# Layer 2 head attention: from scores kept once to two sets of scores

## The reference

```python
x = x + _L2_attn_ref(_layernorm(x, axis=-1), L2_attn_Wq, L2_attn_Wk, L2_attn_Wv, L2_attn_Wo)
...
q, k = _rope(q, k)
scale = 1.0 / np.sqrt(Dh)
scores = jnp.einsum('bqhd,bkhd->bhqk', q, k) * scale
causal = jnp.triu(jnp.ones((S, S), dtype=bool), k=1)
scores = jnp.where(causal, -jnp.inf, scores)
attn = jax.nn.softmax(scores, axis=-1)
out = jnp.einsum('bhqk,bkhd->bqhd', attn, v).reshape(B, S, H * Dh)
return out @ Wo.T
```

## Time and profile before

| | |
|---|---|
| median of 3 runs | 1747.39 us (1744.67 to 1747.46) |
| the profiled execution | 1748.18 us |
| its span | 1746.5 us, 27918 instructions |
| granted TensorE clock, mean | 0.881 |
| PE / DVE / ACT / POOL busy | 76% / 54% / 53% / 23% of the span |
| stage L2a | from 927.0 us to 1149.3 us of the span |

### The profile page before, as it was taken

How to read it: one execution, slowest core, us unless ns; L and a number is a source line. 1 busy time by engine, 2 the same in 40 slices (tenths; PEclk the granted TensorE clock), 3 DMA queues, 4 the chain that set the end, 5 groups by cost and what they waited for, 6 DMA issues and landing times. The chain is left out here.

```text
span 1746.5 us, 27918 instructions
## 1 busy us (share of the span) xinstructions
PE 1328.2 (76%) x9137; PEld 830.3 (48%) x9137; DVE 949.7 (54%) x3708; ACT 927.3 (53%) x2185; POOL 399.7 (23%) x490
## 2 busy tenths in 40 slices
PE   5887888868899999777996878765083567877574
PEld 3555555545444444553563555454063434444464
DVE  4577777754455655445113776647222757666432
ACT  2688878752477776532421766643020467767232
POOL 5433333210311110100004332001544042210134
PEclk9899999988999999887998888886596889999687
DMA  7900000000000000000005000000122000000022
GB/s 210 135 1 2 2 2 1 2 1 1 1 1 1 1 1 1 1 1 1 1 1 178 1 1 2 1 1 11 54 74 79 2 19 14 7 14 1 8 59 78
DMA packets 60263, 42.34 MB, mean 24 GB/s; under 512 B 13188, under 2 KB 54120, under 8 KB 60120
## 3 DMA queue, kind: packets, MB, share of 16 engines
q1 hardware_dynamic: 54752, 32.42, 7.8%
q0 software_dynamic: 3552, 7.33, 1.2%
q10 hardware_dynamic: 1816, 0.81, 0.2%
HBM read 25.88 MB, written 14.66 MB: 23 GB/s over the span
## 5 line engine op out<-in xcount | busy, mean ns | idle before, releaser
L792 ACT ACTIVATE L0a_e<-L0a_e,L0a_neg_max 128x256 f32<-128x256 f32 (+1 forms) x512 | 195.5, 446 | 27.2 <-DVE L0a_neg_max L868 26.4
L679 PE MATMUL L0a_psE<-ident,L0a_e 128*128 128x128 f32 x768 | 119.0, 286 | 58.8 <-DVE L0a_probs L877 42.1
L679 PEld LDWEIGHTS L0a_psE<-ident,L0a_e 128*128 128x128 f32 x768 | 87.3, 145 | 100.8 <-issue 58.7
L1216 DVE CUSTOM_DVE_ANT_0 L3x_e<-L3x_psS,L3x_mask_rows 128x256 f32<-128x256 f32 x256 | 93.4, 420 | 70.2 <-PE L3x_psS L1076 70.0
L1164 ACT ACTIVATE L3x_e<-L3x_e,L3x_neg_max 128x256 f32<-128x256 f32 x256 | 112.6, 503 | 19.1 <-DVE L3x_neg_max L1216 19.1
L792 ACT ACTIVATE L2a_e<-L2a_e,L2a_neg_max 128x128 f32<-128x128 f32 (+1 forms) x256 | 97.3, 445 | 41.4 <-DVE L2a_neg_max L868 41.4
L1084 PE MATMUL L3x_psE<-ident,L3x_e 128*128 128x128 f32 x512 | 76.6, 284 | 47.3 <-DVE scores_L_experts_L L1226 37.1
L868 DVE CUSTOM_DVE_ANT_0 L0a_e<-L0a_psS,trinity 128x128 f32<-128x128 f32 (+1 forms) x256 | 76.3, 353 | 38.5 <-PE L0a_psS L669 26.2
L1084 PEld LDWEIGHTS L3x_psE<-ident,L3x_e 128*128 128x128 f32 x512 | 56.6, 143 | 83.5 <-issue 45.1
L868 DVE CUSTOM_DVE_ANT_0 L2a_e<-L2a_psS,causal_rows 128x128 f32<-128x128 f32 (+1 forms) x256 | 76.0, 353 | 32.4 <-PE L2a_psS L669 26.3
L868 DVE CUSTOM_DVE_ANT_0 L0a_e<-L0a_psS,causal_rows 128x128 f32<-128x128 f32 (+1 forms) x256 | 76.2, 353 | 31.8 <-PE L0a_psS L669 22.2
(11 more groups left out here) (652 smaller groups left out, 3265.2 us busy)
## 6 DMA issues: line engine op xcount, KB each, us to landing
L2f_rows<-packed_rows SPq DMA_DIRECT2D x8, 325.0 KB
packed_rows<-zeros SPq DMA_DIRECT2D x1, 2560.0 KB, 30.9
experts_L_L<-in_L_ffn_w_dram SPq DMA_DIRECT2D x1, 2048.0 KB, 8.3
unpacked_rows<-zeros SPq DMA_DIRECT2D x1, 2048.0 KB, 20.5
scores_L_experts_L<-in_L_ffn_w_dram SPq DMA_DIRECT2D x1, 2048.0 KB, 8.5
L2f_back_rows<-unpacked_rows SPq DMA_DIRECT2D x16, 128.0 KB, 2.6
L3x_mask_rows<-in_mask_Bx1xSxS_ff_dram SPq DMA_DIRECT2D x8, 256.0 KB, 2.7
sorted_rows<-zeros SPq DMA_DIRECT2D x1, 1472.0 KB, 18.3
```

The costliest lines, as they stand in the source:

```text
L679: last = nc.tensor.transpose(psE[i % 2][:, c * P:(c + 1) * P], e[:, i % RING, c * P:(c + 1) * P], mem.ident[:])
L792: last = nc.scalar.activation(at, at, ACT.Exp, bias=neg[:, i % RING, j:j + 1], scale=-1.0)
L1216: last = nc.vector.tensor_tensor_reduce(out=e[:, i % RING, j * S:(j + 1) * S], in0=psS[r][:, j * S:(j + 1) * S], in1=mrow[:, b % 2, t, :], ...
```

## The change

Layer 2's head attention is made by a new function, `split_quads`, in place of `quad_heads`; layers 0 and 3 stay as they are. `split_quads` computes each score twice. The first set (`score`) has queries on the partitions, as before, in the two banks `psS`; a matmul with the mask adds it (`hide_score`); DVE takes four maxima of a bank of 512 (`reduce`) and writes nothing else. Over a batch the maxima are gathered (`gather_max`), turned on PE (`turn_max`) and negated in two bf16 parts (`negate`). The second set (`logits`) has keys on the partitions, in a ring of three banks `psL`: scores, then the negated maximum added by a bf16 matmul over 32 rows (`shift`), then the mask by another (`hide`); ACT takes the exponential of 512 columns from PSUM and writes `probs`. The turning of exponentials and their copies are gone, and so are `e` and the two halves of the copy work.

A batch is six steps `n` of two banks. In step `n` of batch `b` PE issues the logits of that step and the first-set scores of one step of the next batch (number `m`), on the other two quads. POOL makes `qm` as well as `km` (eight masked copies a batch in place of four). Normalising (`next_h`) and `divide` go from POOL to DVE, the copies of `hT` and `raw` from DVE to ACT. The sums and the projection have a bank of their own, `psN`, shared with the turned maxima. Helpers not shown are as in `quad_heads`.

```diff
--- before.py
+++ after.py
@@ -924,6 +924,601 @@
...
+def split_quads(nc, mem, w, name, layers, *, scale, wq_rot=None, wk_rot=None, loads=(), clear=()):
...
+    KINDS = ((0, 0), (1, 0), (1, 1))
+    SLOTS, ITEMS, SLOT = 6, 12, 32
+    RING = 3
+    SCORE_AT = ((0, 0), (2, 0), (2, 1), (2, 2), (0, 1), (0, 2))
...
+        qm, km = sb("qm", [P, 3, 4, S]), sb("km", [P, 3, 4, S])
...
+        psS = [ps("psS0"), ps("psS1")]
+        psL = [ps(f"psL{i}") for i in range(RING)]
+        first_banks = psS + psL[0:2]
+        psO, psM, psN = ps("psO"), ps("psM"), ps("psN")
...
+            @block.gpsimd
+            def _(pool):
+                nc.gpsimd.memset(v[:], 0.0).then_inc(consts, 1)
+                nc.gpsimd.memset(mx[:], 0.0).then_inc(consts, 1)
...
+                def variants(src, dst, b, done):
+                    for j in range(4):
+                        last = nc.gpsimd.tensor_scalar(dst[:, b % 3, j, :], src[:, b % 3, :], w["rows4"][:, j:j + 1], None, ALU.mult)
+                    last.then_inc(done, 1)
+
+                for b in range(NB):
+                    if rope:
+                        pool.wait_ge(s_rq, b + 1)
+                        if b >= 3:
+                            pool.wait_ge(s_score, ITEMS * (b - 2))
+                        nc.gpsimd.tensor_tensor(qT[:, b % 3, :], turned[:, 0, :], turned[:, 1, :], ALU.add).then_inc(s_qT, 1)
+                        pool.wait_ge(s_rk, b + 1)
...
+                            pool.wait_ge(s_logit, ITEMS * (b - 2))
+                        nc.gpsimd.tensor_tensor(kT[:, b % 3, :], turned[:, 2, :], turned[:, 3, :], ALU.add).then_inc(s_kT, 1)
+                    pool.wait_ge(s_kT, b + 1)
+                    if b >= 3:
+                        pool.wait_ge(s_score, ITEMS * (b - 2))
+                    variants(kT, km, b, s_km)
...
+                    variants(qT, qm, b, s_qm)
...
+                def free_score_banks(m):
+                    if m >= 1:
+                        pe.wait_ge(s_red, 2 * m)
+                    if m % SLOTS == 0:
+                        pe.wait_ge(s_km, m // SLOTS + 1)
+
+                def score(m, a):
+                    b, p = divmod(m, SLOTS)
+                    r0, k = SCORE_AT[p]
+                    t, u = KINDS[k]
+                    rows = slice(32 * (r0 + a), 32 * (r0 + a) + 32)
+                    last = nc.tensor.matmul(psS[a][:], qT[rows, b % 3, t * P:(t + 1) * P], km[rows, b % 3, :, u * P:(u + 1) * P],
+                                            start=True, stop=of(b).mask.scores[k] is None, skip_group_check=True)
+                    if of(b).mask.scores[k] is None:
+                        last.then_inc(s_score, 1)
+
+                def hide_score(m, a):
+                    hidden = of(m // SLOTS).mask.scores[SCORE_AT[m % SLOTS][1]]
+                    if hidden is not None:
+                        nc.tensor.matmul(psS[a][:], mem.identb[:], hidden.unsqueeze(1).to_broadcast([P, 4, P]), start=False, stop=True,
+                                         skip_group_check=True).then_inc(s_score, 1)
...
+                def first_scores(k):
+                    if k == 0:
+                        pe.wait_ge(s_km, 1)
+                    else:
+                        pe.wait_ge(s_red, 4 * k)
...
+                    for r in range(4):
+                        rows = slice(32 * r, 32 * r + 32)
+                        last = nc.tensor.matmul(first_banks[r][:], qT[rows, 0, t * P:(t + 1) * P], km[rows, 0, :, u * P:(u + 1) * P],
+                                                start=True, stop=hidden is None, skip_group_check=True)
...
+                def logits(b, n, a):
+                    r, k = 2 * (n // 3) + a, n % 3
+                    bank = psL[(ITEMS * b + 2 * n + a) % RING]
+                    rows = slice(32 * r, 32 * r + 32)
+                    if k < 2:
+                        nc.tensor.matmul(bank[:], kT[rows, b % 3, 0:P], qm[rows, b % 3, 2 * k:2 * k + 2, :],
+                                         start=True, stop=False, skip_group_check=True)
+                    else:
+                        nc.tensor.matmul(bank[:], kT[rows, b % 3, P:S], qm[rows, b % 3, :, P:S],
+                                         start=True, stop=False, skip_group_check=True)
...
+                def shift(b, n):
+                    k = n % 3
+                    for j in range(2 if k < 2 else 4):
+                        for a in range(2):
+                            r = 2 * (n // 3) + a
+                            bank = psL[(ITEMS * b + 2 * n + a) % RING]
+                            rows = slice(32 * r, 32 * r + 32)
+                            if k < 2:
+                                nc.tensor.matmul(bank[:, j * S:(j + 1) * S], w["sel4"][rows, 2 * k + j, :], nm[rows, :],
+                                                 start=False, stop=False, skip_group_check=True)
+                            else:
+                                nc.tensor.matmul(bank[:, j * P:(j + 1) * P], w["sel4"][rows, j, :], nm[rows, P:S],
+                                                 start=False, stop=False, skip_group_check=True)
...
+                def hide(b, n, a):
...
+                        at = bank[:].rearrange("p (a q) -> p a q", a=2)
+                        two = mem.identb[:].unsqueeze(1).to_broadcast([P, 2, P])
+                        last = nc.tensor.matmul(at[:, :, 0:P], mask.near, two, start=False, stop=True, skip_group_check=True)
...
+                    else:
+                        last = nc.tensor.matmul(bank[:], mask.far, mem.identb[:].unsqueeze(1).to_broadcast([P, 4, P]),
+                                                start=False, stop=True, skip_group_check=True)
+                    last.then_inc(s_logit, 1)
...
+                def turn_max(b):
+                    pe.wait_ge(s_mx, b + 1)
...
+                    for t in range(TPB):
+                        last = nc.tensor.transpose(psN[:, t * P:(t + 1) * P], mx[:, t, :, :].rearrange("p r c -> p (r c)"), mem.ident[:])
+                    last.then_inc(s_mxt, 1)
...
+                warm(20)
+                for b in range(2):
+                    turn(b)
+                    warm(3)
+                    queries(b)
+                    warm(5)
+                    if rope:
+                        keys(b)
+                        warm(4)
+                    if b == 1:
+                        first_scores(0)
+                    values(b)
+                    warm(3)
+                turn(2)
+                for k in range(1, 3):
+                    warm(8)
+                    first_scores(k)
+                warm(8)
+                free_score_banks(SLOTS)
+                for a in range(2):
+                    score(SLOTS, a)
+                for a in range(2):
+                    hide_score(SLOTS, a)
+                turn_max(0)
+                for b in range(NB):
+                    for n in range(SLOTS):
+                        m = SLOTS * (b + 1) + n + 1
+                        i = ITEMS * b + 2 * n
+                        ahead = m < SLOTS * NB
+                        if n == 0:
+                            pe.wait_ge(s_qm, b + 1)
+                        if i + 2 > RING:
+                            pe.wait_ge(s_prob, i + 2 - RING)
+                        if ahead:
+                            free_score_banks(m)
+                        for a in range(2):
+                            logits(b, n, a)
+                        if ahead:
+                            for a in range(2):
+                                score(m, a)
+                            for a in range(2):
+                                hide_score(m, a)
+                        if n == 0:
+                            pe.wait_ge(s_nm, b + 1)
+                        shift(b, n)
+                        for a in range(2):
+                            hide(b, n, a)
+                        if n == 0:
+                            if b + 2 < NB:
+                                queries(b + 2)
+                            if b > 0:
+                                weigh(b - 1, 2)
+                        if n == 1:
+                            if b + 2 < NB and rope:
+                                keys(b + 2)
+                            if b > 0:
+                                weigh(b - 1, 3)
+                        if n == 2:
+                            if b + 2 < NB:
+                                values(b + 2)
+                            if b > 0:
+                                spread_sums(b - 1)
+                        if n == 3:
+                            weigh(b, 0)
+                        if n == 4:
+                            if b > 0:
+                                project(b - 1)
+                            weigh(b, 1)
+                        if n == 5:
+                            if b + 1 < NB:
+                                turn_max(b + 1)
+                            if b + 3 < NB:
...
+                for b in range(NB):
```

(74 more changed lines are left out.)

299 lines of the change are left out of this document (added).

## The result

The changed kernel takes 1730.16 us (median of 4 runs, 1727.0 to 1733.5) beside 1747.13 us for the kernel before (4 runs, 1744.67 to 1747.46): a ratio of 0.9905, 95% interval 0.989 to 0.9919, so 17 us less. Its profiled span is 1727.5 us.

A forecast was written before the change was run, and what follows sets the result against it. Old L2a bound by two round trips per batch border, the new by PE at 22 us a batch. Start 963.4 + 171.8 = 1135.2, 14.1 less; clock costs 3.4, so gain 10.7: median 1737, range 1724 to 1758 (own range 1731 to 1743).

The forecast's parts named there:

- n3: Step of a batch with logits, scores, shift, `hide` and weigh: 2.59 us, with no other batch work.
- n4: Step of a batch with a masked score, shift, `hide`, `project` 1.08 and weigh: 4.11 us.
- n5: Last step of a batch: 4.15 us, as DVE's `reduce` waits for `turn_max`; PE stands 1.7 us, eight times.
- n1: Step of a batch with logits, scores, shift, `hide`, `keys` 0.86 and weigh: 3.45 us.
- its sign of PE standing in other steps: Sign of a wrong root: steps held by `hide_score`, two reductions and the way to PE; 0.3 us spare without filler.
- Shift: Bf16 matmul over 32 rows in each step: 0.23 + 3 x 0.09 = 0.50 us, between 0.23 and 0.80.
- Rival (3): Tiling-mode changes drain PE, 0.17 us each, a shift costs 0.97: 1758 us, chance 0.12; at 0.80, 1750, chance 0.12.
- rival (2): Shift and its neighbours overlap wholly, 0.23 us each, `raw` copies 20.5 apart: 12 us less, 1722, chance 0.14.
- The fill: Start of L2a: first reduction at 949.6, first logits at 963.4, 8 us later than now; clearing `v` first returns 4.2.
- The clock: PE's granted clock in the new L2a: 0.98, costing 0.02 x 172 = 3.4 us.
- Rival (4): Clock stays at 0.86 because of PE's stand in n5: 24 us more, 1761, chance 0.12.
- these two round trips: Old L2a's batch borders: PE stands 17.6 us for copies of turned exponentials and 12.6 for the division.

The follow-up runs named there:

- two_mx: The changed kernel with two copies of the maxima tile `mx`, by parity of the batch: ratio to the kernel before 0.9866, L2a 199.11 us.
- hide_twice: The changed kernel with the same mask added twice to each logits bank: ratio to the kernel before 0.9988, L2a 220.98 us.
- after_again: The changed kernel run a second time, unedited: ratio to the kernel before 0.9920, L2a 210.35 us.
- grouped_two_mx: two_mx with `shift` moved directly behind the scores, ahead of `hide_score`, in steps n1 to n5: ratio to the kernel before 0.9868, L2a 197.86 us.
- clear_first: The kernel before, with POOL clearing `v` at the start of L2a ahead of the normalised rows: ratio 0.9953, L2a 216.38 us.
- l0_split: The changed kernel with layer 0's two attentions made by `split_quads` as well: ratio to the kernel before 1.0034, L2a 207.29 us.
- divide_early: The kernel before, with POOL's division in L2a put between its two additions, ahead of the masked copies: ratio 0.9883, L2a 202.95 us.
- filled: The kernel before, with ten useless bf16 matmuls ahead of `project` in L2a: ratio 1.0000, L2a 221.23 us.
- quads_mended: The kernel before with the edits of divide_early and of clear_first, the latter in layer 0 too: ratio 0.9805, L2a 196.22 us.

## Why the prediction was right, point by point

**The forecast's mechanism held.** PE paces the new form at 21.8 us a batch (22.0 forecast) with nothing else full. Two_mx takes a stand out and gains, hide_twice puts work in and pays 1.5 of 1.8 us. The stage was 209.3 us long by its first and last instruction (1133.86 - 924.56) against 222.3 - 10.7 = 211.6 forecast. The median of 1730.2 lies 1 us under the forecast's own range of 1731 to 1743; of the 6.3 us between the gain forecast and the one measured, 2.3 are in the stage, and the rest outside it came only in part in after_again.

**The steps.** Measured against forecast, from the starts 1010.68, 1014.46, 1017.09, 1021.03, 1025.33, 1029.24 and 1032.50 of PE's timeline: n2 3.78 (3.84), n3 2.63 (2.59), n4 3.94 (4.11), n5 4.30 (4.15), n0 3.91 (3.89), n1 3.26 (3.45). The sum 21.82 is near by errors against each other: n1 and n4 were 0.36 too dear, n5 0.15 too cheap, and n3 was right by luck. By its own rows n3 has 0.97 + 0.31 + 0.23 + 0.79 = 2.30 of work. It takes 2.63 because the next step waits for n3's two reductions (the 0.17 at 1017.09), which is the 2.6 that the prediction had worked out as the least that they allow. This is, in small, its sign of PE standing in other steps.

**Shift was over-sized.** 0.50 forecast. It takes 0.31 to 0.33, and 0.09 more for the mask ahead of it; where no mask stands between, the scores ahead take 0.97 and not 1.07, so that it adds 0.21 in all. Three changes of kind were charged to it. Two show in a masked step, 0.09 on the mask ahead and 0.08 to 0.10 over the 0.23 in shift itself; in an unmasked one the second is there and the scores ahead give 0.10 back. Rival (3), the drain at 0.17 and more, is refuted by these rows and by grouped_two_mx; rival (2), whole overlap, was near the truth for the unmasked steps and gave no 20.5, as n5's stand was there and n3 is held by its reductions.

**n5 was under-sized by 0.15.** The transposes' start to DVE's reduction is 1023.90 - 1023.41 = 0.49 where I had 0.35. PE stands 1.3 to 1.5 us, six times, not 1.7 and eight: the 1.7 had the 0.25 of the transposes in it, which is PE's work, so that the sum itself held a stand of 1.4; and the last two borders have no scores to wait for. That I took the wait on `mx` as given is a larger miss than its size: two_mx shows 11.2 us behind a term that the sum had priced, with the clock that fell behind it.

**The fill** came 36.9 us for 36.4 (its terms add up to 36.1: 949.6 + 2.4 + 2 x 3.7 + 0.2 + 3.5 = 963.1, not 963.4). Clearing `v` first gave 4.3 back (clear_first), for 4.2.

**The clock cost what was forecast, in another way.** I took 0.98, 3.4 us spread over the loop. From 961 to 1134 us the mean was 0.97 (0.98 in after_again), and nearly all of the loss lies in two first steps of a batch, each behind a stand of 1.54 us:

```profile
1090.77 0.97 PE L1159 MATMUL L2a_psL<-L2a_qm,L2a_kT 32*128 32x512 f32 x2 [1.54 <-DVE L2a_mx L1446]
...
1095.36 0.70 PE L1159 MATMUL L2a_psL<-L2a_qm,L2a_kT 32*128 32x512 f32 x2
```

This step takes 4.59 us and the first of the loop 4.65 (961.44 to 966.09), where two_mx at full clock has 3.05 and 3.13: 3.1 us in all. Behind the five stands of 1.32 us the clock stayed at 1.00. Rival (4) fell with it. The length of a stand does not settle it by itself. In l0_split the same loop begins behind the same 1.54 us, and its first step runs at full clock, 3.12 us; with 1.5 us more ahead of the loop that is the 3.0 us by which L2a is shorter there:

```profile
986.50 0.70 PE L1159 MATMUL L2a_psL<-L2a_qm,L2a_kT 32*128 32x512 f32 x2 [1.54 <-DVE L2a_mx L1446]
...
989.62 0.70 PE L1159 MATMUL L2a_psL<-L2a_qm,L2a_kT 32*128 32x512 f32 x2
```

**Where the 2.3 us lie.** From the first loop matmul to the end 172.4 us passed. Without the 3.1 of clock that is 169.3, where the sum at full clock was 171.8: batches 1 to 5 took 109.1 for 110 (981.71 to 1090.77), batch 6 18.0 for 18.3, and batch 7 up to its last step 13.1 for 14.3 (1110.33 to 1123.45). The over-sized shift is a part of that; the rest I did not divide.

**"The stage is bound by these two round trips" was half right, and named without its cause.** The division's round trip was the bound: divide_early moves one instruction and the batch falls from 25.3 to 20.35. The prediction took the 12.6 us that PE stood for its price, 2.5 a batch, and 4.9 came back. By filled some 1.2 to 1.7 of that is clock. The rest fits DVE's queue behind `project` (its wait fell from 18.4 us to 4.6), but no run parts DVE's share from PE's. The copies' round trip was not: its stands stay when the batch is 5 us shorter. What bounds quads_mended is open; DVE is busy 17.2 of 21 us there, PE 17.5, and no run tells its queue and the `psE` stands apart.

**What the change itself is worth.** Nothing in the runs shows two sets of scores to be better or worse in this stage than one: mended each in its own way, L2a takes 198.5 and 196.2 us. The gain of 13.0 can be had without the new form: it also took the division off POOL and cleared `v` first, and these two alone give the old form 27.1. In layer 0, with no additions on POOL, the new form loses 22 us.

## What to carry to other kernels

Before a stage is rewritten because an engine stands, look what the releasing engine did just ahead of the release, in its own queue: here an instruction of 1.3 us stood 5.8 us, behind a wait for the keys and 3.6 us of copies for two batches later, and moving it was worth more than the rewrite. A stage of the same code that runs faster elsewhere in the same trace (L0a at 20.5, L2a at 25.3 us a batch) is the sign to look for. And price the engines queued behind a late result, not only the one that the prediction looks at: PE stood 2.5 us a batch for the division, DVE up to 3.9 for the projection behind it, and 4.9 came back.
